# Three attention stages of a fused transformer kernel: another source for the softmax sums of two steps, another order at a batch's ends, and a new order in the third attention

## The reference, cut to what matters

```python
def attention(x, W_qkv, W_out):                       # layers 0, 2 and 3; b = one sequence
    q, k, v = split_heads(x @ W_qkv)                  # 16 heads of 64 (layers 0, 3) or of 16 (layer 2)
    if layer == 3: q, k = layernorm(q) * g + b, layernorm(k) * g + b     # over the 64 channels of a head
    s = einsum('bqhd,bkhd->bhqk', q, k) * D ** -0.5
    if layer == 2: s = where(mask, s, -inf)
    p = softmax(s)                                    # exp(s - max), divided by its sum over keys
    o = einsum('bhqk,bkhd->bqhd', p, v)
    return o.reshape(...) @ W_out + b_out
```

## Time and profile before

| what | us |
|---|---|
| median of three executions | 3338.05 |
| lowest, highest | 3335.65, 3476.47 |
| the profiled execution: its own time | 3335.07 |
| its span | 3333.3 |
| TensorE busy | 3028.1 (91%) |
| VectorE busy | 2154.0 (65%) |
| ScalarE busy | 1694.8 (51%) |
| GpSimd busy | 915.1 (27%) |

### The profile page before, as it was taken

One profiled execution on the slowest core, in us unless ns is written; L12 is line 12 of the kernel. 1 busy time (PEld: TensorE's weight loads), 2 busy tenths in 40 slices (PEclk: granted clock), 3 DMA queues, 4 the chain that ended last, 5 costly groups with the idle time before them and its releaser, 6 DMA issues. The chain is left out here.

```text
span 3333.3 us, 70757 instructions
## 1 busy us (share of the span) xinstructions
PE 3028.1 (91%) x26089; PEld 2516.2 (75%) x26090; DVE 2154.0 (65%) x4193; ACT 1694.8 (51%) x3085; POOL 915.1 (27%) x725
## 2 busy tenths in 40 slices
PE   7999999997998989999999699799999999994697
PEld 5887888775998979877777598577777777772586
DVE  4655565655666766567777566757575757567775
ACT  3444444443554445554455345566666666662364
POOL 2232323232112231122222211322222222221574
PEclk8999999998999999999999799899999999997799
DMA  5000000001001000000000100100000000004243
GB/s 171 4 6 6 6 3 6 6 6 36 19 19 46 0 23 0 22 4 9 9 9 9 46 19 19 36 1 0 0 0 0 0 0 0 0 1 130 80 126 86
DMA packets 68976, 80.66 MB, mean 24 GB/s; under 512 B 10146, under 2 KB 61090, under 8 KB 68884
## 3 DMA queue, kind: packets, MB, share of 16 engines
q1 hardware_dynamic: 62756, 71.14, 7.4%
q0 software_dynamic: 6144, 8.52, 1.4%
HBM read 66.80 MB, written 12.85 MB: 24 GB/s over the span
## 5 line engine op out<-in xcount | busy, mean ns | idle before, releaser
L956 POOL TENSOR_TENSOR L3a_shift<-L3a_neg,L3a_mx 128x256 fp32r<-128x256 f32 x128 | 94.7, 740 | 523.1 <-DVE L3a_mx L1556 523.1
L1063 ACT ACTIVATE L0a_prob<-L0a_st 128x512 f32<-128x512 f32 x256 | 134.0, 602 | 160.4 <-PE L0a_st L1293 72.6
L945 POOL TENSOR_TENSOR L0a_o<-L0a_prob 128x1024 f32<-128x1024 f32 x48 | 118.8, 2475 | 302.6 <-PE L0a_o L1330 302.6
L1063 ACT ACTIVATE L3a_prob<-L3a_st 128x512 f32<-128x512 f32 x256 | 133.8, 602 | 117.8 <-POOL L3a_o L945 90.0
L1925 ACT ACTIVATE L2a_prob<-L2a_st 128x512 f32<-128x512 f32 x256 | 132.2, 604 | 117.7 <-PE L2a_st L1958 117.7
L1556 DVE TENSOR_REDUCE L0a_mx<-L0a_s 128x2 f32<-128x512 f32 x224 | 143.8, 683 | 73.9 <-PE L0a_s L1267 73.9
L1546 DVE SCALAR_TENSOR_TENSOR L3a_qk_lo<-raw,cols_sb,L3a_qk_hi 128x256 fp32r<-128x256 f32 x256 | 157.9, 656 | 36.5 <-ACT L3a_qk_hi L1054 36.5
L1556 DVE TENSOR_REDUCE L3a_mx<-L3a_s 128x2 f32<-128x512 f32 x256 | 163.7, 679 | 15.5 <-PE L3a_s L1267 15.5
L2190 DVE TENSOR_REDUCE L2a_mx<-L2a_s 128x2 fp32r<-128x512 f32 x256 | 163.5, 681 | 15.2 <-PE L2a_s L1958 15.2
L1157 PE MATMUL L0a_st<-L0a_xt,home 128*128 128x256 f32 x512 | 150.1, 293 | 5.1 <-DVE home L1664 5.1
L1158 PE MATMUL L0a_st<-L0a_xt,home 128*128 128x256 f32 x512 | 145.6, 284 | 0.0
(11 more groups left out here) (615 smaller groups left out, 11241.6 us busy)
## 6 DMA issues: line engine op xcount, KB each, us to landing
raw<-in_moe_w SPq DMA_DIRECT2D x16, 1024.0 KB, 8.6
x_sb<-in_x SPq DMA_DIRECT2D x1, 4096.0 KB, 24.9
L0a_gate<-gate_rows SPq DMA_DIRECT2D x32, 128.0 KB, 3.9
L0m_gate<-gate_rows SPq DMA_DIRECT2D x32, 128.0 KB, 3.8
L2a_gates<-gate_rows SPq DMA_DIRECT2D x32, 128.0 KB, 3.9
L2m_gate<-gate_rows SPq DMA_DIRECT2D x32, 128.0 KB, 3.8
out_x<-x_sb SPq DMA_DIRECT2D x1, 4096.0 KB, 17.0
token_rows<-x_sb SPq DMA_DIRECT2D x1, 4096.0 KB, 29.3
```

Of the source, the lines that this page charges most:

```text
L945: nc.gpsimd.tensor_tensor(half_sums, both[:, :, :, 0:N], both[:, :, :, N:2 * N], ALU.add).then_inc(halves_done, 1)
L956: nc.gpsimd.tensor_tensor(shift[:, u % 4, :, :, :], neg64[:].unsqueeze(1).unsqueeze(1).to_broadcast([P, 2, TT, 64]), mx[:, u % 2, :, :].un ...
L1063: A(prob[:, u % 4, h, :], st_ps[u % 2][h][:], ACT.Exp, scale=64 ** -0.5).then_inc(p_done, 1)
```

## The change

In `heads64` (L0a and L3a):

- GpSimd makes the halves of pair 2 alone. ScalarE no longer waits for halves before the exponentials of pairs 2 and 3. The sums of pairs 0 and 1 run over all exponentials (eight matmuls in place of four), behind the `column_part` of their own pair.
- At a batch's end the order is `qk(0)`, `sums(3)`, `sums(2)`, `column_part(3)`: the sums are complete ahead of the last value products.
- L3a only: ScalarE's `qn_high(0)` moves from behind `raw_copy(6)` to behind `raw_copy(7)`; VectorE's `moments` is cut in two, and its second part (`spreads`) goes behind `row_both`; `last_o_low(0)` goes ahead of `modulate`.

In `heads16` (L2a):

- The transposed scores of a unit's two pairs are interleaved, so that matmuls to all four row groups follow each other; in unit 1 the pairs stay apart, with the wait for `xlo_done` between them. In unit 3 the wait for `taken` now stands ahead of both pairs.
- In unit 1 TensorE's `over` goes from ahead of `qk` to behind `max_rows`. VectorE's `over` goes behind `shift` and `qk_low`, `x_low` from the end of unit 0 to between the two heads of `maxes` in unit 1, `o_low(0)` from unit 1 to unit 2, `o_low(1)` of unit 2 one place back. ScalarE's `o_high(0)` goes behind `qk_high`.

```diff
@@ heads64, GpSimd, L3a and L0a
                     for u in range(6):
                         shift_of(i, u)
-                    halves(i, 0)
                     shift_of(i, 6)
                     shift_of(i, 7)
-                    halves(i, 1)
                     halves(i, 2)
...
-                    for p in range(3):
-                        halves(i, p)
+                    halves(i, 2)
                     tail(i)
@@ heads64, ScalarE
-                        if c >= 6:
-                            qn_high(c - 6)
+                        if c == 7:
+                            qn_high(0)
+                            qn_high(1)
...
-                    if p in (2, 3):
-                        act.wait_ge(halves_done, 3 * i + p - 1)
@@ heads64, TensorE
                     if halved:
-                        pe.wait_ge(halves_done, 3 * i + p + 1)
+                        pe.wait_ge(halves_done, i + 1)
...
-                                          start=(p == 0), stop=(p == 2), skip_group_check=True)
+                                          start=(p == 0 and kt == 0), stop=(p == 2), skip_group_check=True)
...
                     row_part(p)
-                    if p >= 2:
-                        sums(p - 2, True)
                     column_part(p - 1)
+                    if p < 3:
+                        sums(p - 1, False)
...
                     qk(0, i + 1)
                 sums(3, False)
+                sums(2, True)
                 column_part(3)
-                sums(2, True)
@@ heads64, VectorE
                     V.bn_stats(stats[:, tt, :], tile(j * TT + tt)).then_inc(stats_done, 1)
+
+            def spreads(j):
+
                 for tt in range(TT):
                     dve.wait_ge(stats_done, TT * j + tt + 1)
...
                     moments(i + 1)
+                    if not qknorm:
+                        spreads(i + 1)
...
                 if not first:
                     row_both(i - 1)
+                if qknorm and not final:
+                    spreads(i + 1)
...
                     last_over(1)
+                    last_o_low(0)
                     if not final:
                         modulate(i + 1)
-                    last_o_low(0)
@@ heads16, ScalarE
-                    if u == 1 and not first:
-                        o_high(i - 1, 0)
                     if u == 0 or not final:
                         qk_high(U * i + u + 3, (u + 3) % U, 0)
...
                     if u == 1 and not first:
+                        o_high(i - 1, 0)
                         o_high(i - 1, 1)
@@ heads16, TensorE
-                def scores_t(w):
+                def scores_t(u, pairs):
...
-                            for h in range(2):
-                                last = mm(st_ps[w % 2][h][:, kt * N:(kt + 1) * N], ...
+                            for w in pairs:
+                                for h in range(2):
+                                    last = mm(st_ps[w][h][:, kt * N:(kt + 1) * N], ...
...
-                    scores_t(2 * u)
                     if u == 1 and not final:
+                        scores_t(u, (0,))
                         pe.wait_ge(xlo_done, i + 2)
-                    if u == 3 and not first:
-                        pe.wait_ge(taken, i)
-                    scores_t(2 * u + 1)
+                        scores_t(u, (1,))
+                    else:
+                        if u == 3 and not first:
+                            pe.wait_ge(taken, i)
+                        scores_t(u, (0, 1))
...
-                    if u == 1 and not first:
-                        pe.wait_ge(p_done, 4 * slot + 3)
-                        over(i - 1, 0)
-                        over(i - 1, 1)
...
                         max_rows(u + 1)
+                    if u == 1 and not first:
+                        pe.wait_ge(p_done, 4 * slot + 3)
+                        over(i - 1, 0)
+                        over(i - 1, 1)
@@ heads16, VectorE
-                    if ahead:
+                    if ahead and u == 1 and not final:
+                        maxes(2 * slot + 2, 2 * u + 2, (0,))
+                        x_low(i + 1)
+                        maxes(2 * slot + 2, 2 * u + 2, (1,))
+                    elif ahead:
                         maxes(2 * slot + 2, 2 * u + 2)
...
                     if u == 2 and not first:
-                        o_low(i - 1, 1)
+                        o_low(i - 1, 0)
...
+                    if u == 2 and not first:
+                        o_low(i - 1, 1)
+                    if ahead:
+                        shift(slot + 1, (u + 1) % U)
+                    if u == 0 or not final:
+                        qk_low(U * i + u + 3, (u + 3) % U, 0)
                     if u == 1 and not first:
                         over(i - 1, 0)
                         over(i - 1, 1)
-                    if ahead:
-                        shift(slot + 1, (u + 1) % U)
-                    if u == 1 and not first:
-                        o_low(i - 1, 0)
-                    if u == 0 or not final:
-                        qk_low(U * i + u + 3, (u + 3) % U, 0)
-                    if u == 0 and not final:
-                        x_low(i + 1)
```

More of the change, by code:

```diff
@@ L1656, in _ @@
             moments(0)
+            spreads(0)
             normalise(0)
@@ L2032, in scores_t @@
                         for n, (a, b) in enumerate(((qk_hi, qk_hi), (qk_lo, qk_hi), (qk_hi, qk_lo))):
-                            for h in range(2):
-                                last = mm(st_ps[w % 2][h][:, kt * N:(kt + 1) * N], a[rows(w, h), w // 2, ks], b[rows(w, h), w // 2, 0:N],
-                                          start=(kt == 0 and n == 0), stop=(n == 2))
-                                if kt == TT - 1 and n == 2:
-                                    last.then_inc(st_done, 1)
+                            for w in pairs:
+                                for h in range(2):
+                                    last = mm(st_ps[w][h][:, kt * N:(kt + 1) * N], a[rows(w, h), u, ks], b[rows(w, h), u, 0:N],
+                                              start=(kt == 0 and n == 0), stop=(n == 2))
+                                    if kt == TT - 1 and n == 2:
+                                        last.then_inc(st_done, 1)
                 def values():
@@ L2183, in qk_low, with maxes @@
                 V.tensor_tensor(qk_lo[:, c, :], ring[bank][:], qk_hi[:, c, :].bitcast(F32), ALU.subtract).then_inc(qklo_done, 1)
-            def maxes(pair, w):
-                for h in range(2):
+            def maxes(pair, w, heads=(0, 1)):
+                for h in heads:
                     dve.wait_ge(s_done, 2 * pair + h + 1)
```

## The result

The changed kernel takes 3294.79 us (median of four executions, 3294.43 to 3301.59) where the kernel before took 3336.85 beside it; the ratio is 0.988, 95% interval 0.9861 to 0.990. The forecast was 3311 us with a range of 3288 to 3328: the range holds the time, the forecast was 16 us too high. The profiled execution has a span of 3293.1 us for 3333.3.

The account below looks back on a forecast made before the run. TensorE was taken to set the pace, the gain being its standing time less added matmuls. Per batch L3a -0.29, L0a -0.12, L2a -1.15, together -1.56 us over 15 steps, -23.4: 3335 - 24 = 3311 us, range 3288 to 3328.

Parts of the forecast that it names:

- unit 2 waits for VectorE's `over`: L2a: unit 2's scores wait for VectorE's two over, now behind shift and qk_low, yet start 1.13 us earlier.
- The rival that the interleaving is on the path: L2a: interleaved transposed scores win 0.3 us in three units of 15 batches, 13.5 us, giving 3297; chance 0.13.
- Part 1: L0a and L3a, sums of pairs 0 and 1: matmuls +0.86 us a batch, halves' waits -1.14 (L3a), -0.80 (L0a).
- the start of a batch: L0a: small hand-overs at the transposes and next block go, -0.25 us a batch, against +0.07 for sums(2).
- the new stop: L0a and L3a: sums(2), ahead of column_part(3), waits for GpSimd's halves 0.05 to 0.2 us, taken as +0.07.
- Part 3: L3a, qn_high(0) behind raw_copy(7): VectorE's qk_scaled(1) comes later, so qk_scale(3) and later steps wait, +1.18 us a batch.
- The rival that the moved copies cost nothing: L3a: VectorE's order leaves slack, so moving qn_high(0) gives -0.53 us a batch, total 3285; chance 0.13.
- The start of an L3a batch: L3a: the stops ahead of over(0) and project(0) go, -0.75 us a batch, bounds 0 and -1.0.
- the stop ahead of `scores(6)`: L3a: TensorE's 0.5 us wait for VectorE's maxima of unit 5 is covered by the longer sums, -0.51 a batch.
- "nothing comes": Stage ends win nothing: L0a's VectorE is busy with next-stage weights; L3a's sums(2) waits for halves.
- VectorE was not the bound: Rival that VectorE is the bound: L2a gives 0, L3a +0.97 us a batch, total 3348; chance 0.07.
- L2a's gain was not eaten: Rival that in L2a the wait for VectorE's over in unit 2 eats the gain, +17 us, total 3328; chance 0.13.

Follow-up runs that it names:

- e4_pairs_apart: Changed kernel with L2a's transposed scores of a unit's two pairs one after another again in units 0, 2 and 3: 3297.33 us.
- e8_before_sums: Kernel before, with only the sums of pairs 0 and 1 over all exponentials and GpSimd halves of pair 2 alone, in L0a and L3a: 3314.9 us.
- e3_halves_back: Changed kernel with GpSimd's halves of pairs 0 and 1, ScalarE's waits and sums over halves restored in L0a and L3a: 3318.58 us.
- e5_values_first: Changed kernel with column_part(3) ahead of sums(2) again in L0a and L3a, VectorE's new order kept: 3299.13 us.
- e1_high_early: Changed kernel with L3a's ScalarE qn_high(0) back in its old place behind raw_copy(6): 3279.68 us.
- e7_vector_order: Changed kernel with VectorE's old order at an L3a batch's start (all moments ahead of row_both, o_low(0) behind modulate), new sums order kept: 3303.05 us.
- e6_spare_adds: Changed kernel with two more GpSimd additions in L3a, sized and placed like the old halves, on unchanging output weights, results unused: 3303.41 us.
- e11_over_back: Changed kernel with L2a's over back ahead of qk on TensorE and ahead of shift and qk_low on VectorE: 3307.52 us.

## Why the prediction was right, and where it was short

**L2a: right**, -1.15 for -1.27. `over` behind `max_rows` 0.81, `x_low` 0.44, interleaving 0.10: 1.35 one by one, 1.27 together. The step "unit 2 waits for VectorE's `over`" held, TensorE in units 1 and 2, kernel after:

```profile
1633.57 0.40 PE L1961 MATMUL L2a_s<-L2a_qk_hi 32*128 32x256 f32 x4
...
1635.85 0.33 PE L1961 MATMUL L2a_st<-L2a_rsum_hi,L2a_spread 128*128 128x256 f32 x1
...
1637.38 1.07 PE L1961 MATMUL L2a_o<-L2a_prob,L2a_v 128*32 128x256 f32 x16
1638.54 0.39 PE L1961 MATMUL L2a_st<-L2a_qk_hi 32*128 32x256 f32 x4
...
1639.65 0.50 PE L1961 MATMUL L2a_s<-L2a_qk_hi 32*128 32x256 f32 x4
```

and VectorE's `over` there:

```profile
1637.12 1.27 DVE L2162 TENSOR_TENSOR L2a_o<-L2a_o_raw,L2a_st 128x512 f32<-128x512 f32 x2
```

It ends at 1638.39, TensorE starts unit 2 at 1638.54, 0.16 later than the 1.00 us that `weighted` takes unheld (the earlier trace rows has that distance for sixteen records). From the start of unit 1 to that of unit 2 it is 1.13 us less than before, the forecast number. The block of transposed scores, "x4" throughout, is followed by the next block 1.11 us after its start in this unit (1.20 before) and 0.92 in unit 0 (1.25 before). The rival that the interleaving is on the path is out: e4_pairs_apart gives it 0.10 a batch where the rival needs 0.9, for in unit 0 the gain goes again before unit 1, which starts 0.27 later against the reciprocal. That the rival's time, 3297, lies nearest to the measured one is an accident. The Trainium skill's 3.07 times ("TensorE: Matmul & The Clock Gate", the measured speedup against the span model) would have made it the likely one; here it gave 1.4 (1.25 us to 0.92) in the one unit where nothing held the block, for the old order had its fours together half of the time. Its PSUM Bottleneck ("TensorEngine Tiling (Array Packing)") is what the trace agrees with: in units 2 and 3 the `scores` behind the block wait for VectorE's maxima, which read PSUM, and of 1.20 us 1.11 were left.

**L0a: right within its batches**, -0.12 for -0.10. Part 1 forecast at +0.06 is worth 0.00 to 0.03 (e8_before_sums, e3_halves_back); the start of a batch, forecast at -0.18 with the new stop, gave 0.10 (e5_values_first). How its last batch ends was wrong, see below.

**Part 3: right.** +1.18 forecast, +1.12 by e1_high_early. The stop and its releaser are as written. Counted from `project(0)`, `qk_scale(3)` starts 0.52 us later than before (forecast 0.6); its stop is 0.89 and not 0.6, since the variances ahead of it start 0.44 earlier. The rival that the moved copies cost nothing is out.

**The start of an L3a batch: right in kind, undersized, and put down to the wrong edit.** From the next batch's `qk(1)` to `project(0)` TensorE took 8.01 us before, 6.99 after: -1.02, the lower bound given, for -0.75. I had `o_low(0)` start 6.44 after `qk(1)`, it did at 6.16: VectorE's two `over` follow each other without a gap, where I let the second wait for TensorE as before. And the prediction put the gain down under the new place of `sums(2)`, though the steps it names are VectorE's. e5_values_first shows that undoing the place of `sums(2)` costs 0.04 in L3a and 0.10 in L0a: VectorE's own two moves carry 0.9 without it. Undoing those two costs 0.46 (e7_vector_order): the sums' place alone carries the rest, since it too frees `over(0)`. The new stop of 0.07 ahead of `sums(2)` was there, 1.07 us for 1.00.

**Part 1: the term that was mis-sized.** -0.79 forecast in L3a, -1.35 measured twice. The waits for the halves (-1.17 with hand-overs) and the stop ahead of `scores(6)` (-0.44 of idle time) came as forecast. What the sum lacked are 0.5 us inside the row parts of pairs 2 and 3, where no row shows a wait. Timeline of TensorE, pair 2, kernel before, then after:

```profile
2326.22 0.50 PE L1267 MATMUL L3a_s<-L3a_qk_hi 64*128 64x256 f32 x4 [0.44 <-DVE L3a_mx L1556]
...
2327.28 0.28 PE L1293 MATMUL L3a_st<-L3a_shift,ones_r 64*128 64x256 f32 x2
2327.47 0.38 PE L1287 MATMUL L3a_st<-L3a_qk_hi 64*128 64x256 f32 x2
```

```profile
2300.95 0.50 PE L1263 MATMUL L3a_s<-L3a_qk_hi 64*128 64x256 f32 x4
...
2302.01 0.29 PE L1289 MATMUL L3a_st<-L3a_shift,ones_r 64*128 64x256 f32 x2
2302.13 0.28 PE L1283 MATMUL L3a_st<-L3a_qk_hi 64*128 64x256 f32 x2
...
2303.32 0.28 PE L1289 MATMUL L3a_st<-L3a_shift,ones_r 64*128 64x256 f32 x2
```

Before, the next product after the first subtraction starts 0.19 us behind it, after, 0.12. There are four places in this row part where the same 0.07 or more is lost, and from `scores(6)` to the last subtraction (2328.92) it is 2.70 us before and 2.37 after; in pair 3 the same difference is 0.19. Pair 1, in which TensorE still comes straight out of a stop behind VectorE's maxima, has 0.19 in both kernels. For the first of these places VectorE's rows show the wait: `scores_t(5)` needs the low part of unit 5, the second of the two here. Kernel before, then after:

```profile
2326.09 1.23 DVE L1546 SCALAR_TENSOR_TENSOR L3a_qk_lo<-raw,cols_sb,L3a_qk_hi 128x256 fp32r<-128x256 f32 x2
```

```profile
2300.33 1.23 DVE L1545 SCALAR_TENSOR_TENSOR L3a_qk_lo<-raw,cols_sb,L3a_qk_hi 128x256 fp32r<-128x256 f32 x2
```

Before, it ended at 2327.32, 0.15 us ahead of the product that needs it (2327.47); after, at 2301.56, 0.57 ahead of it (2302.13). So there the sums, 1 us more of TensorE's own work, hide a wait for VectorE that was too short to stand in a row. The result of e6_spare_adds, which keeps the sums and has the short distances in pair 2, fits; that the other three places have the same cause is argued and not shown.

**The ends of the stages: "nothing comes" was wrong for L0a.** From the start of the last batch's `qk(1)` to the first row of the next stage it took 74.5 us before (751.28 to 825.75) and 69.6 after (750.19 to 819.82). I had written that VectorE is busy there with the next stage's weights. It is, but it is so for as long as GpSimd lets it be. Last batch of L0a, kernel before, VectorE, GpSimd and TensorE:

```profile
782.73 3.42 DVE L259 TENSOR_TENSOR home<-L0a_w_stage,home 128x1024 fp32r<-128x1024 f32 x1
```

```profile
782.54 2.52 POOL L945 TENSOR_TENSOR L0a_o<-L0a_prob 128x1024 f32<-128x1024 f32 x1 [13.55 <-PE L0a_o L1330]
```

```profile
787.40 0.63 PE L1267 MATMUL L0a_s<-L0a_qk_hi 64*128 64x256 f32 x4 [2.83 <-DVE L0a_mx L1556]
```

Kernel after, VectorE, the same instruction:

```profile
781.62 1.22 DVE L259 TENSOR_TENSOR home<-L0a_w_stage,home 128x1024 fp32r<-128x1024 f32 x1
```

The addition of the halves keeps VectorE's subtraction from ending for 2.2 us, the maxima stand behind it, and TensorE stands for 2.83. With the halves back (e3_halves_back) the subtraction takes 3.42 again and the same stretch 72.9 us; with part 1 alone (e8_before_sums) it takes 69.7. The change removes the addition, not only the wait for it. This accounts for 3.3 of the 4.9 us. The other 1.6 are TensorE's clock: behind the stop the kernel before ran at a granted clock of 0.51 for 3.5 us (columns as in the earlier trace rows), and e3_halves_back, with the same stop, did not. Kernel before, a stretch and the value products in it, then the same products in e3_halves_back:

```profile
787.60:791.10 3.50, 3.50 (x24) 1.71 (x24) 3.05 (x5) 1.08 (x2) 0.00 (x0) 0.51 0.41 137
789.19 2.84 PE L1330 MATMUL L0a_o<-L0a_prob,L0a_v 128*64 128x256 f32 x16
```

```profile
785.57 1.95 PE L1331 MATMUL L0a_o<-L0a_prob,L0a_v 128*64 128x256 f32 x16
```

**The sum.** From TensorE's first row of one stage to that of the next, L0a came out 5.9 us shorter (forecast 1.8), L2a 17.1 (17.3; what its batches won beyond that, it gave back at its end) and L3a 16.8 (4.4): 12.4 and 4.1 us are the 16 that were missing. L3a's 0.89 more a batch: 0.56 in part 1, 0.27 at the start, 0.06 in part 3. All three errors lie on one side, none hid another. VectorE was not the bound: L2a won 1.27 a batch and the stop ahead of `scores(6)` went, where that rival had both stay; its busy time fell by 25 us for the same work. L2a's gain was not eaten either. One reading of the prediction was wrong without weight: the profiled execution, 3335.07, lies below the lowest of the runs it names (3335.65), not between that and the median.

## What to carry to other kernels

A move on one engine has its sign from the lists of the others: read who is queued between the moved result and its user (here one VectorE instruction made 0.45 us won into 1.12 lost), and change both lists together. When a chain is freed, look for the second edit that frees it too before giving either the credit. Time an engine's work by what runs beside it: an addition that nobody waits for can still hold up another engine's instruction.

## What the runs showed of the hardware

**GpSimd's addition stops VectorE's instructions that read two operands in SBUF.** 1.22 us became 3.42 for the subtraction of 128x1024 elements beside an addition of 2.52, and in every batch one `qn_low` of 0.47 became 1.40 (1.80 once); e6_spare_adds had the 1.40 too, with an addition that shares no data with VectorE's work. Maxima, which read PSUM, kept their 0.68. The Trainium skill says so ("SBUF — State Buffer", who interferes with whom): a VectorE instruction with two inputs in SBUF contends with a GpSimd instruction that reads SBUF, the shared port pair is an exclusive lock, and on trn2 a `tensor_reduce` never contends. The trace agrees, 3.42 being nearly what is left of the addition (2.33) and 1.22 behind it, and shows it for a `scalar_tensor_tensor` as well, whose two tensor operands here were both in SBUF.

**One batch of L2a in the kernel before ran at a lower clock.** Stretches of the kernel before: us, busy of PE, PEld, DVE, ACT, POOL, granted clock, DMA share, GB/s:

```profile
1642.23:1650.65 8.42, 7.74 (x83) 6.19 (x84) 6.74 (x10) 4.83 (x11) 3.58 (x5) 1.00 0.11 31
1650.65:1654.65 4.00, 4.00 (x21) 4.00 (x21) 2.23 (x4) 1.07 (x2) 0.00 (x0) 0.57 0.00 0
1654.65:1672.54 17.89, 17.49 (x209) 13.49 (x209) 12.26 (x24) 8.59 (x16) 4.38 (x4) 1.00 0.00 0
```

For 4 us the granted clock was 0.57 of 2.4 GHz, most of them at the lower level of 1.2; it fell within `over`, 0.5 us behind the longest stop of the batch, for the third exponential (0.46, as in the earlier trace rows), and the batch took 30.31 us where its neighbours took 28.77. The same happened to one batch of e11_over_back (29.81 for 28.31) and to two of e8_before_sums, which have that stop, and to no regular batch of the other ten experiments and of the kernel after, which have not. So the change saved some 1.5 us in the regular batches by this as well; why it takes one batch and not the others stays open. In the last batch the kernel after lost more than that again. The last distance of reciprocals in L2a, kernel before, then after:

```profile
1845.23:1875.84 30.61, 21.23 (x227) 15.96 (x225) 19.15 (x31) 14.83 (x26) 6.98 (x6) 0.84 0.09 26
```

```profile
1818.71:1852.19 33.48, 21.85 (x227) 15.90 (x227) 19.43 (x30) 15.30 (x27) 7.23 (x7) 0.81 0.08 24
```

It is 2.9 us longer: the granted clock is 0.81 for 0.84, and TensorE's stops in it, behind VectorE's maxima and ScalarE's exponentials for the most part, sum to 10.6 us for 8.2.
